# Two Trainium2 routing hand-overs: first-layer expert weights released in halves, and a GpSimd bias add moved behind them

## The chip, the cores and the metric

The kernel runs on one core of one Trainium2 chip. The metric is device time in microseconds (us) of one execution; lower is better. The five engines run their own instruction streams and meet only through semaphores: TensorE (PE in the profile; its weight loads are PEld), VectorE (DVE), ScalarE (ACT), GpSimd (POOL) and SyncE (SP), which issues the transfers.

## The reference, cut to what matters

The input x is 4 rows (sequences) of 512 tokens with 512 features. The model is a block of two feed-forward layers around an attention-like layer:

```
x = x + 0.5 * ffn(layernorm(x))
x = x + attn(layernorm(x))
x = x + 0.5 * ffn(layernorm(x))

ffn(x):
    logits = x.reshape(4, 512*512) @ switch_w.T + switch_b     # one routing decision per row
    gate, top_idx = top_k(softmax(logits), 2)                  # 2 of 8 experts per row
    for each of 16 heads of 32 features and both chosen experts k:
        h = gelu(x_head @ w1[k].T + b1[k])                     # 32 -> 32
        o += gate[k] * (h @ w2[k].T + b2[k])                   # 32 -> 32
    return (x + o) @ w3.T + b3
```

So each feed-forward layer begins with a routing decision that needs the whole normalised input, and no expert matmul can start before the decision for its row is known.

## The kernel before, in words

**Precision.** Matmuls are made of three products: an operand is split in a rounded high part (type `F32R`) and the remainder, its low part, and hi*hi, hi*lo and lo*hi are summed in PSUM.

**The two routings.** All four rows are routed together. In the first phase `route(0)` multiplies the normalised x with `switch_w` (512 matmuls); VectorE's `choose` then reads the result from PSUM, sums it (`part`, L1254), spreads it by row (`lmix`, L1255), TensorE sums over the partitions (L571), and `choose` goes on to `place`, the rank of each expert in each row. ScalarE takes the exponential meanwhile. `select(row, f, 0)` then picks the first-layer weights of the row's two experts from a table and writes them as a block diagonal for two heads at a time; `select(row, f, 1)` does the same for the second layer, and its column 32 is the bias b1 (semaphore `s_b1`). `gate`, called in the middle of it, makes the gates. The third phase, with the second feed-forward layer, repeats all this after the attention of the last row as `route(1)`, `logits(1)`, `choose(1)`.

**Feed-forward work.** f counts the feed-forward layers of rows: 0 to 3 the first, 4 to 7 (B = 4 and more, "late") the second. The features lie in KC = 4 chunks c of 128. TensorE's `hidden(f, c)` makes the hidden values of both experts in two PSUM banks: two matmuls for each of its three products. ScalarE's `gelu` reads them (it needs `s_b1`), `second_hi` or `hidden_hi` rounds; VectorE's `split_hidden` (f below 4) casts `h_hi` of k = 0 (L1357) and subtracts for `h_lo` (L1358, twice), `hidden_lo` does the subtractions alone (L1364). TensorE's `experts_out(f, c)` (O0 to O3; L436 to L438, six matmuls each) waits for `s_hl`, one count for each `h_lo`. `z_out` on ScalarE and `z_split` on VectorE (L1376) bring its result out of PSUM, and `w3_tile` (W0 to W3) multiplies by w3. VectorE's `w3_add` (L1383) adds what GpSimd has left in `xa`.

**What GpSimd does here.** `residual_bias(f, t)` (L1148) adds half of b3 to a 128x512 tile of the normalised layer's input, in place, and signals `s_xb`, which `w3_add` waits for. In the first routing its four adds for f = 0 start as soon as the last tile is normalised; for f = B they start when the four `xt_lo` tiles of that layer are written.

**Order of the work.** Each engine's order is written out by hand. Around the first routing VectorE does: `route_norm`, four `xt_split`, `choose(0)`, `select(0, 0, 0)`, `select(0, 0, 1)` with `gate(0)`, `split_hidden(0, 0)`, `split_hidden(0, 1)`, the low part of w3 (`w3_lo`, L1513, 128x2048), then `split_hidden(0, 2)`, `z_split(0, 0)`, `split_hidden(0, 3)` and the other `z_split`. TensorE does: `hidden(0, 0)`, `hidden(0, 1)`, O0, `hidden(0, 2)`, O1, `hidden(0, 3)`, O2, six matmuls of `w3_ahead`, O3, `w3_behind`. Around the second routing VectorE does: `choose(1)`, `select(0, B, 0)`, `select(0, B, 1)`, `hidden_lo(B, 0)`, `normalise(B + 1, 1)` (L1337), `hidden_lo(B, 1)`, `z_split(B, 0)`, `select(1, B + 1, 0)`, `hidden_lo(B, 2)`, `z_split(B, 1)`, `xt_split`, `select(1, B + 1, 1)`, `hidden_lo(B, 3)`.

**Steps.** `own.do(ins)` issues a VectorE instruction and waits for it on VectorE's own semaphore; `own.mark` only counts it. `VE_ROW_STEPS` is the count of such steps in the loop over the middle rows.

Of the kernel before, what the change touches and what calls it, by code (L numbers as in the profile page):

```python
# [31 lines left out]
P = 128  # L32
ALU = mybir.AluOpType
# [6 lines left out]
B, S, D = 4, 512, 512  # L40
NT = S // P
KC = D // P
E, TOPK = 8, 2
HD = 32
# [12 lines left out]
PAIR = 2  # L57
# [33 lines left out]
def macaron_kernel(nc, x, w_in, w_out, switch_w, tables_in, w3, out):  # L91
    x2_dram = nc.dram_tensor("x2_dram", (B, S, D), F32).ap()

    with ExitStack() as ctx:
        def sb(name, shape, dt=F32, into=ctx):
            return into.enter_context(nc.sbuf_tensor(name, shape, dt))

        def sem(name):
            return ctx.enter_context(nc.semaphore(name))
# [43 lines left out]
        with ExitStack() as region:  # L143
# [4 lines left out]
            w_diag = sb("w_diag", [P, TOPK, PAIR, HD], into=region)  # L148
# [12 lines left out]
        xt_hi = sb("xt_hi", [P, KC, S], F32R)  # L161
        xt_lo = sb("xt_lo", [P, KC, S], F32R)
# [43 lines left out]
        pair_of = sb("pair_of", [P, PAIR])  # L206
# [31 lines left out]
        def weights(of):  # L238
# [3 lines left out]
                    xt_lo=xt_lo, prod=prod, w_diag=w_diag)  # L242
        late0 = dict(ffn0, prod=prod_late, w_diag=w_diag_late)
        late1 = dict(weights(set1), z_hi=z_hi1, z_lo=z_lo1, xt_hi=xt_hi1,
                     xt_lo=xt_lo1, prod=prod_late, w_diag=w_diag_late)
# [6 lines left out]
        def is_late(f):  # L252

            return isinstance(f, int) and f >= B

        def ffn_set(f):
            return (late1 if f % 2 else late0) if is_late(f) else ffn0
# [69 lines left out]
        s_sh = sem("s_sh")  # L327
        s_exp = sem("s_exp")
        s_sel = [sem("s_sel1"), sem("s_sel2")]
        s_b1 = sem("s_b1")  # L330

        s_xn = sem("s_xn")
# [7 lines left out]
        s_hl = sem("s_hl")  # L340
# [81 lines left out]
        def normed(n):  # L422

            _, t, lo, hi = EVENTS[n]
            if n < FEW + 2:
                return n + 1
            assert n >= LAST
            return n - 1
# [111 lines left out]
        def _(pe):  # L540
# [56 lines left out]
            def hidden(f, c, after_row):  # L597
                use = ffn_set(f)
                if c == 0:
                    pe.wait_ge(s_sel[0], f + 1)  # L600
                pe.wait_ge(s_t1e, KC * f + c + 1)
                pe.wait_ge(s_xtl, KC * f + c + 1)
                for k in range(PAIR):
                    if after_row is not None and c == 0:
                        pe.wait_ge(s_ina, OUT_JOBS * after_row + 15 + k)
                    elif not (isinstance(f, int) and f == 0 and c == 0):
                        pe.wait_ge(s_gelu, H_JOBS * f + PAIR * (c - 1) + k + 1)
                half = [slice(k * HALF, (k + 1) * HALF) for k in range(PAIR)]
                dst = [h_bank[k][:] for k in range(PAIR)]
                for k in range(PAIR):  # L610
                    pe.matmul(dst[k], use["w1_hi"][half[k], :], use["xt_hi"][half[k], c, :], start=True, stop=False)  # L611
                for k in range(PAIR):
                    pe.matmul(dst[k], use["w1_lo"][half[k], :], use["xt_hi"][half[k], c, :], start=False, stop=False)
                for k in range(PAIR):
                    pe.matmul(dst[k], use["w1_hi"][half[k], :], use["xt_lo"][half[k], c, :], start=False,  # L615
                              stop=True).then_inc(s_h, 1)

            def experts_out(f, c):
# [129 lines left out]
            def row_end(b):  # L748
# [24 lines left out]
                t1(f, 2, b, False)  # L773
                t1(f, 3, b, False)
                hidden(f, 0, b)
                for name in ("A0", "A1"):
                    do(name, range(KC - 1, KC))
                hidden(f, 1, b)
                do("A2", range(1))
                do("O0")  # L780
                hidden(f, 2, b)
                do("O1")
                hidden(f, 3, b)
# [313 lines left out]
        def _(pool):  # L1097
            own = Steps(pool, s_po)
# [45 lines left out]
            def residual_bias(f, t):  # L1144

                ap = ffn_input(f)[0][:, t, :]
                pool.wait_ge(s_xn, NT * f + t + 1)
                pool.tensor_tensor(ap, ap, b3_half, ALU.add).then_inc(s_xb, 1)  # L1148
# [16 lines left out]
            pool.wait_ge(s_b3, 1)  # L1165
            pool.wait_ge(s_x0, NT - 1)
            pool.wait_ge(s_rn, normed(NT - 1))
            for t in range(NT):
                residual_bias(0, t)
            ln_rstd(0)  # L1170
# [11 lines left out]
            pool.memset(set1[4][:].bitcast(F32), 0.0).then_inc(s_pad, 1)  # L1182
            pool.memset(set1[5][:].bitcast(F32), 0.0).then_inc(s_pad, 1)
            pool.wait_ge(s_xtl, KC * (B + 1))
            for c in range(KC):
                residual_bias(B, c)
            for f in range(B + 1, 2 * B):
# [9 lines left out]
        def _(ve):  # L1197
            own = Steps(ve, s_ve)
# [6 lines left out]
            def route_stats(n):  # L1205

                phase, t, lo, hi = EVENTS[n]
                src = route_src(n)
                if lo == 0:
                    if phase == 0:  # L1210
                        ve.wait_ge(s_xc[t], 16)
                    else:
                        ve.wait_ge(s_xr[t % 2], 16 * (t // 2 + 1))
                for b in range(lo, hi):
                    m = own.mark(ve.bn_stats(stats[:, b, :], src(b)))
                return m
# [72 lines left out]
            def select(row, f, n, gates=lambda: None):  # L1289

                use = ffn_set(f)
                w_diag = use["w_diag"]
                if n == 0:
                    prod, out = use["prod"][:, :, 0:HD, :], use["sel"][0]
                    for k in range(TOPK):
                        m = own.mark(ve.scalar_tensor_tensor(
                            out=prod[:, k], in0=place[:, bass.ds(row, 1), :].to_broadcast([P, HD, E]),
                            scalar=float(k), in1=tab[0][:, 0:HD, :], op0=ALU.is_equal, op1=ALU.mult))
                    own.wait(m)
                    for k in range(TOPK):  # L1300
                        m = own.mark(ve.tensor_reduce(out[:, k, :], prod[:, k], AX.X, ALU.add))
                    own.wait(m)
                    for k in range(TOPK):
                        m = own.mark(ve.tensor_tensor(
                            w_diag[:, k], out[:, k, :].unsqueeze(1).to_broadcast([P, PAIR, HD]),
                            pair_of[:].unsqueeze(2).to_broadcast([P, PAIR, HD]), ALU.mult))
                    own.wait(m)
                    full = w_diag[:].rearrange("p k j c -> p (k j c)")
                    hi, lo = use["w1_hi"][:], use["w1_lo"][:]
                else:  # L1310
                    prod, out = use["prod"][:, 0], use["sel"][1]
                    own.do(ve.scalar_tensor_tensor(
                        out=prod, in0=place[:, bass.ds(row, 1), :].to_broadcast([P, FB, E]), scalar=half_of[:],
                        in1=tab[1], op0=ALU.is_equal, op1=ALU.mult))
                    ve.tensor_reduce(out[:], prod, AX.X, ALU.add).then_inc(s_b1, 1)
                    gates()
                    ve.wait_ge(s_b1, f + 1)
                    own.do(ve.scalar_tensor_tensor(
                        out=w_diag[:, 0], in0=out[:, 0:HD].unsqueeze(1).to_broadcast([P, PAIR, HD]),
                        scalar=gate_p[:, bass.ds(row, 1)], in1=pair_of[:].unsqueeze(2).to_broadcast([P, PAIR, HD]),  # L1320
                        op0=ALU.mult, op1=ALU.mult))
                    if is_late(f):
                        ve.wait_ge(s_pad, 2)
                    full = w_diag[:, 0].rearrange("p j c -> p (j c)")
                    hi, lo = use["w2_hi"][:, 1, :], use["w2_lo"][:, 1, :]
                    if not isinstance(f, int):
                        own.mark(ve.tensor_copy(b2_row[:], b2_col[:, bass.ds(row, 1)]))
                own.do(ve.tensor_copy(hi, full))
                ve.tensor_tensor(lo, full, hi, ALU.subtract).then_inc(s_sel[n], 1)  # L1329
                ve.wait_ge(s_sel[n], f + 1)  # L1330

# [174 lines left out]
            ve.wait_ge(s_pc, 1)  # L1506
            choose(0)
            select(0, 0, 0)
            select(0, 0, 1, lambda: gate(0))
            split_hidden(0, 0, None)  # L1510
            split_hidden(0, 1, None)
# [63 lines left out]
            with ve.Fori(1, B - 1) as b:  # L1575
                own.base, own.n = base + (b - 1) * VE_ROW_STEPS, 0
                row(b)
                assert own.n == VE_ROW_STEPS, own.n

            own.base, own.n = base + (B - 2) * VE_ROW_STEPS, 0  # L1580

# [11 lines left out]
            for t in range(NT):  # L1593
                out_add(t, job_last(f"A{t}"), last_bank[t], x1, x1)
                ve.wait_ge(s_obf, job_last(f"A{t}") + 1)
                m = route_stats(LAST + t)
# [41 lines left out]
                w3_add(2 * B - 1, t, job_late(2 * B - 1, f"W{t}"), out_bank(f"W{t}"))  # L1638


VE_ROW_STEPS = 56


# [34 lines left out]
```

## Time and profile before

| | us |
|---|---|
| median of 3 runs (lowest, highest) | 535.35 (534.96, 535.4) |
| the profiled execution's own time | 535.08 |
| its span in the trace | 533.3 |
| TensorE matmul busy | 487.2 (91% of the span) |
| VectorE busy | 415.1 (78%) |
| ScalarE busy | 220.0 (41%) |
| GpSimd busy | 104.1 (20%) |

The span is that of the instructions in the trace; 1.8 us of the execution's time lie around it. A row of the timeline gives the start in us from the span's start, the duration in us, the engine, line, operation, tiles and forms, and how many instructions were merged in the row; in brackets stands the idle time of the engine before it and what ended it. The granted clock of TensorE is given as a share of full speed: 1.00 is 2.4 GHz, 0.50 is 1.2 GHz.

### The profile page before, as it was taken

The numbers are of one execution on the slowest core, as the hardware profiler recorded it, in microseconds if no ns is written. First come the engines' busy times: TensorE is split into PE (matmuls) and PEld (weight loads), VectorE is DVE, ScalarE is ACT, GpSimd is POOL, SyncE is SP. The second block draws the span as 40 slices with busy tenths as digits, with TensorE's granted clock in tenths as the row PEclk, the third lists the DMA queues.
The fourth block names the chain that finished last, engine by engine and source line by source line (L and its number), as shares of the span: only waits on it lengthen the run. The fifth ranks groups of instructions, "written<-read, shape, count | busy, mean of one in ns | idle before, by whom it ended". The sixth has DMA issues, their size and how long they took to land.

```text
span 533.3 us, 8582 instructions
## 1 busy us (share of the span) xinstructions
PE 487.2 (91%) x3184; PEld 353.9 (66%) x3204; DVE 415.1 (78%) x801; ACT 220.0 (41%) x352; POOL 104.1 (20%) x116
## 2 busy tenths in 40 slices
PE   0566999999999999999999999999999748999997
PEld 0553676667687666768666677866667635777775
DVE  3878888999875599887569979758997679878642
ACT  0226753444714222572422257141344238665630
POOL 5150036000013500001440000154121320021220
PEclk9786999999999999999999999999999978999999
DMA  8999020000102000010200001034665060131112
GB/s 335 409 371 417 10 79 2 1 1 0 41 20 100 0 1 0 2 40 21 98 0 0 0 0 39 20 138 166 235 226 202 4 206 33 41 111 47 60 59 80
DMA packets 16370, 48.19 MB, mean 90 GB/s; under 512 B 1232, under 2 KB 1232, under 8 KB 14544
## 3 DMA queue, kind: packets, MB, share of 16 engines
q1 hardware_dynamic: 16336, 47.73, 24.2%
q8 instruction: 22, 0.36, 0.3%
q14 instruction: 12, 0.10, 0.1%
HBM read 39.34 MB, written 8.39 MB: 89 GB/s over the span
## 4 chain that ended last, share of the span: by engine, by line
PE 73%; DVE 12%; issue 5%; SPq 3%; DMA 3%; POOL 2%; ACT 1%; POOLq 0%; DVEq 0%; ACTq 0%
PE bank L436 11%; PE bank L438 10%; PE bank L437 10%; PE bank L739 8%; PE bank L740 8%; PE bank L742 8%; DMA route_w<-in_switch_w 3%; SPq L462 2%; PE bank L611 2%; PE bank L593 2%; PE bank L703 2%; PE bank L706 2%; PE bank L711 2%; PE bank L562 2%; POOL rs L1159 2%
## 5 line engine op out<-in xcount | busy, mean ns | idle before, releaser
L739 PE MATMUL bank<-xh,win_hi 128*128 128x512 f32 x256 | 112.6, 440 | 0.0
L740 PE MATMUL bank<-xl,win_hi 128*128 128x512 f32 x256 | 100.6, 393 | 0.0
L742 PE MATMUL bank<-xbf,win_lo 128*128 128x512 bf16 x240 | 65.9, 381 | 1.0
L739 PEld LDWEIGHTS bank<-xh,win_hi 128*128 128x128 f32 x256 | 48.2, 188 | 15.9 <-DVE qn L1447 0.2
L1153 POOL TENSOR_TENSOR rstd<-mv,neg_half 128x1 f32<-128x1 f32 x16 | 9.6, 597 | 246.1 <-DVE mv L1408 246.1
L740 PEld LDWEIGHTS bank<-xl,win_hi 128*128 128x128 f32 x256 | 48.2, 188 | 10.1
L1159 POOL TENSOR_TENSOR rs<-ms,neg_half 128x16 f32<-128x16 f32 x16 | 46.6, 2933 | 23.9 <-DVE ms L1442 23.9
L436 PE MATMUL bank<-w_hi,z_hi 128*128 128x512 f32 x124 | 50.1, 404 | 0.0
L438 PE MATMUL bank<-w_hi,z_lo 128*128 128x512 f32 x124 | 48.5, 391 | 0.0
L437 PE MATMUL bank<-w_lo,z_hi 128*128 128x512 f32 x124 | 48.5, 391 | 0.0
L742 PEld LDWEIGHTS bank<-xbf,win_lo 128*128 128x128 bf16 x256 | 21.1, 98 | 30.7 <-issue 17.4
L877 ACT ACTIVATE hf<-bank,w_sel 128x512 f32<-128x512 f32 x52 | 33.0, 687 | 13.3 <-PE bank L615 9.6
L1148 POOL TENSOR_TENSOR xa<-xa,tables 128x512 f32<-128x512 f32 x16 | 20.2, 1278 | 63.4 <-DVE x L1383 46.2
L1383 DVE TENSOR_TENSOR x<-bank,xa 128x512 f32<-128x512 f32 x28 | 19.3, 690 | 16.2 <-PE bank L438 16.2
L902 ACT ACTIVATE z_hi<-bank,b_col 128x512 fp32r<-128x512 f32 x24 | 16.5, 686 | 31.2 <-PE bank L438 31.2
L436 PEld LDWEIGHTS bank<-w_hi,z_hi 128*128 128x128 f32 x124 | 23.3, 188 | 8.5 <-issue 4.0
L928 ACT ACTIVATE xh<-bank 128x512 fp32r<-128x512 f32 x16 | 9.6, 600 | 46.2 <-PE bank L692 46.2
L1376 DVE SCALAR_TENSOR_TENSOR z_lo<-bank,b_col,z_hi 128x512 fp32r<-128x512 f32 x24 | 17.9, 749 | 13.3 <-ACT z_hi L902 13.1
L611 PE MATMUL bank<-xt_hi,w_hi 64*128 64x512 f32 x64 | 17.5, 542 | 11.7 <-DVE w_lo L1329 8.6
L436 PE MATMUL bank<-wo_hi,y_hi 128*128 128x512 f32 x64 | 27.0, 421 | 0.0
L942 ACT ACTIVATE y_hi<-yt 128x512 fp32r<-128x512 f32 x16 | 10.1, 631 | 40.8 <-DVE yt L1478 40.8
L438 PEld LDWEIGHTS bank<-w_hi,z_lo 128*128 128x128 f32 x124 | 23.3, 188 | 5.2
(217 smaller groups left out, 1060.2 us busy)
## 6 DMA issues: line engine op xcount, KB each, us to landing
route_w<-in_switch_w SPq DMA_DIRECT2D x14, 512.0 KB, 14.0
route_w<-in_switch_w SPq DMA_DIRECT2D x5, 1024.0 KB, 4.7
xa<-in_x SPq DMA_DIRECT2D x4, 1024.0 KB, 5.2
route_w<-in_switch_w SPq DMA_DIRECT2D x2, 2048.0 KB, 15.6
out<-x SPq DMA_DIRECT2D x16, 256.0 KB, 2.0
x_dram<-x1p SPq DMA_DIRECT2D x12, 256.0 KB, 2.0
xa<-x_dram SPq DMA_DIRECT2D x3, 1024.0 KB, 5.7
x_chunk<-in_x SPq DMA_DIRECT2D x2, 1024.0 KB, 17.7
```

The lines of the kernel that those rows point to most:

```text
L436: pe.matmul(res, a_hi, b_hi, start=start, stop=False, skip_group_check=onto)
L437: pe.matmul(res, a_hi, b_lo, start=False, stop=False, skip_group_check=onto)
L438: return pe.matmul(res, a_lo, b_hi, start=False, stop=stop, skip_group_check=onto)
L611: pe.matmul(dst[k], use["w1_hi"][half[k], :], use["xt_hi"][half[k], c, :], start=True, stop=False)
L739: pe.matmul(bank[:], win_hi[:, c, r, k, :], xh[:, k, :], start=(k == 0), stop=False)
L740: pe.matmul(bank[:], win_hi[:, c, r, k, :], xl[:, k, :], start=False, stop=False)
L742: mm = pe.matmul(bank[:], win_lo[:, c, r, k, :], xbf[:, k, :], start=False, stop=(k == KC - 1))
L877: act.activation(hid_set(f, c)[0][:, k, :], h_bank[k][:], ACT.Gelu, bias=ffn_set(f)["sel"][1][:, HD:FB]).then_inc(s_gelu, 1)
L1148: pool.tensor_tensor(ap, ap, b3_half, ALU.add).then_inc(s_xb, 1)
L1159: pool.tensor_tensor(rs[:, t, :], ms[:, t, :], neg_half[:], ALU.pow).then_inc(s_rs, 1)
L1376: ve.scalar_tensor_tensor(out=use["z_lo"][:, c, :], in0=bank[:], scalar=b2_of(f), in1=use["z_hi"][:, c, :], op0=ALU.add, op1=ALU.subtract) ...
L1383: ve.tensor_tensor(x1[:, t, :], bank[:], ffn_input(f)[0][:, t, :], ALU.add).then_inc(s_obf, 1)
```

## The change

Three things are changed.

1. `select(..., 0)` wrote the masked selection to `w_diag` with two instructions of 128x64 (one for each expert), cast it into `w1_hi`, subtracted for `w1_lo`, and signalled once. Now one instruction over 128x128 writes the masked product directly to `w1_hi` (rounded on the way out) and signals a new semaphore `s_sel1h`; a second one writes the same product unrounded to `w_diag`, and the subtraction follows.
2. `hidden` waits for `s_sel1h` before its first matmuls, does hi*hi and hi*lo(x) first and waits for `s_sel[0]` before the two matmuls with `w1_lo`, which come last.
3. GpSimd's four adds of b3 for f = 0 wait in addition until four `h_lo` tiles are written, and those for f = B until `normalise(B + 1, 1)` is done.

```diff
             def hidden(f, c, after_row):
                 use = ffn_set(f)
                 if c == 0:
-                    pe.wait_ge(s_sel[0], f + 1)
+                    pe.wait_ge(s_sel1h, f + 1)
...
                 for k in range(PAIR):
                     pe.matmul(dst[k], use["w1_hi"][half[k], :], use["xt_hi"][half[k], c, :], start=True, stop=False)
                 for k in range(PAIR):
-                    pe.matmul(dst[k], use["w1_lo"][half[k], :], use["xt_hi"][half[k], c, :], start=False, stop=False)
+                    pe.matmul(dst[k], use["w1_hi"][half[k], :], use["xt_lo"][half[k], c, :], start=False, stop=False)
+                if c == 0:
+                    pe.wait_ge(s_sel[0], f + 1)
                 for k in range(PAIR):
-                    pe.matmul(dst[k], use["w1_hi"][half[k], :], use["xt_lo"][half[k], c, :], start=False,
+                    pe.matmul(dst[k], use["w1_lo"][half[k], :], use["xt_hi"][half[k], c, :], start=False,
                               stop=True).then_inc(s_h, 1)
...
             pool.wait_ge(s_b3, 1)
             pool.wait_ge(s_x0, NT - 1)
             pool.wait_ge(s_rn, normed(NT - 1))
+            pool.wait_ge(s_hl, 2 * TOPK)
             for t in range(NT):
                 residual_bias(0, t)
...
             pool.wait_ge(s_xtl, KC * (B + 1))
+            pool.wait_ge(s_xn, NT * (B + 2))
             for c in range(KC):
                 residual_bias(B, c)
...
                         m = own.mark(ve.tensor_reduce(out[:, k, :], prod[:, k], AX.X, ALU.add))
                     own.wait(m)
-                    for k in range(TOPK):
-                        m = own.mark(ve.tensor_tensor(
-                            w_diag[:, k], out[:, k, :].unsqueeze(1).to_broadcast([P, PAIR, HD]),
-                            pair_of[:].unsqueeze(2).to_broadcast([P, PAIR, HD]), ALU.mult))
-                    own.wait(m)
+                    wide = [P, TOPK, PAIR, HD]
+                    columns = out[:].unsqueeze(2).to_broadcast(wide)
+                    own_half = pair_of[:].unsqueeze(1).unsqueeze(3).to_broadcast(wide)
+                    hi, lo = use["w1_hi"][:], use["w1_lo"][:]
+                    ve.tensor_tensor(hi.rearrange("p (k j c) -> p k j c", k=TOPK, j=PAIR), columns, own_half,
+                                     ALU.mult).then_inc(s_sel1h, 1)
+                    own.do(ve.tensor_tensor(w_diag[:], columns, own_half, ALU.mult))
                     full = w_diag[:].rearrange("p k j c -> p (k j c)")
-                    hi, lo = use["w1_hi"][:], use["w1_lo"][:]
+                    ve.wait_ge(s_sel1h, f + 1)
...
-                own.do(ve.tensor_copy(hi, full))
+                if n == 1:
+                    own.do(ve.tensor_copy(hi, full))
                 ve.tensor_tensor(lo, full, hi, ALU.subtract).then_inc(s_sel[n], 1)
...
-VE_ROW_STEPS = 56
+VE_ROW_STEPS = 54
```

## Rows read from the trace of the kernel before

**Rows 1.** The page: busy time, and engines in the chain that ended last.
```profile
PE 487.2 (91%) x3184; PEld 353.9 (66%) x3204; DVE 415.1 (78%) x801; ACT 220.0 (41%) x352; POOL 104.1 (20%) x116
...
PE 73%; DVE 12%; issue 5%; SPq 3%; DMA 3%; POOL 2%; ACT 1%; POOLq 0%; DVEq 0%; ACTq 0%
```

**Rows 2.** Windows: stretch, length, PE, PEld, DVE, ACT, POOL busy (count), PEclk, DMA, GB/s.
```profile
43.30:50.90 7.60, 6.06 (x18) 3.54 (x18) 6.42 (x20) 3.79 (x6) 0.00 (x0) 0.50 1.02 430
...
444.00:455.00 11.00, 9.51 (x52) 6.62 (x51) 10.65 (x24) 10.62 (x20) 0.00 (x0) 1.00 0.01 2
```

**Rows 3.** Timeline of POOL and DVE around both routings' b3 adds.
```profile
33.55 4.95 POOL L1148 TENSOR_TENSOR xa<-xa,tables 128x512 f32<-128x512 f32 x4 [1.88 <-DVE xnr L1241]
...
37.25 1.26 POOL L1148 TENSOR_TENSOR xa<-xa,tables 128x512 f32<-128x512 f32 x1
...
33.24 2.47 DVE L1369 TENSOR_TENSOR xt_lo<-bank,xt_hi 128x512 fp32r<-128x512 f32 x4
...
38.01 0.55 DVE L1255 TENSOR_TENSOR lmix<-part,row_of 128x32 f32<-128x32 f32 x1
...
424.62 4.94 POOL L1148 TENSOR_TENSOR xa<-xa,tables 128x512 f32<-128x512 f32 x4 [4.28 <-DVE xt_lo L1369]
...
428.94 0.67 DVE L1255 TENSOR_TENSOR lmix<-part,row_of 128x32 f32<-128x32 f32 x1
```

**Rows 4.** Timeline of DVE, first routing.
```profile
40.18 0.19 DVE L1268 TENSOR_TENSOR lg<-lg,red 128x32 f32<-128x32 f32 x1
...
42.33 0.36 DVE L1304 TENSOR_TENSOR w_diag<-w_sel,pair_of 128x64 f32<-128x64 f32 x2
42.72 0.23 DVE L1328 CAST w_hi<-w_diag 128x128 fp32r<-128x128 f32 x1
42.98 0.29 DVE L1329 TENSOR_TENSOR w_lo<-w_diag,w_hi 128x128 fp32r<-128x128 f32 x1
...
43.84 0.43 DVE L1315 TENSOR_REDUCE w_sel<-prod 128x33 f32<-128x264 f32 x1
...
48.86 0.43 DVE L1357 CAST h_hi<-hf 128x512 fp32r<-128x512 f32 x1 [0.63 <-ACT hf L877]
...
50.78 2.28 DVE L1513 SCALAR_TENSOR_TENSOR w_lo<-w_raw,w_hi 128x2048 fp32r<-128x2048 f32 x1
52.98 0.42 DVE L1357 CAST h_hi<-hf 128x512 fp32r<-128x512 f32 x1
53.43 1.31 DVE L1358 TENSOR_TENSOR h_lo<-hf,h_hi 128x512 fp32r<-128x512 f32 x2
```

**Rows 5.** Timeline of PE, first routing.
```profile
43.33 0.79 PE L611 MATMUL bank<-xt_hi,w_hi 64*128 64x512 f32 x2 [4.31 <-DVE w_lo L1329]
...
48.06 0.79 PE L436 MATMUL bank<-h_hi,w_hi 128*128 128x512 f32 x1
...
54.35 0.50 PE L436 MATMUL bank<-h_hi,w_hi 128*128 128x512 f32 x1
...
57.65 0.39 PE L436 MATMUL bank<-h_hi,w_hi 128*128 128x512 f32 x1
```

**Rows 6.** Timeline of POOL and DVE in the first row's attention.
```profile
83.22 3.39 POOL L1159 TENSOR_TENSOR rs<-ms,neg_half 128x16 f32<-128x16 f32 x1
...
80.34 2.90 POOL L1159 TENSOR_TENSOR rs<-ms,neg_half 128x16 f32<-128x16 f32 x1 [0.36 <-DVE ms L1442]
...
81.57 2.29 DVE L1486 TENSOR_TENSOR win_lo<-raw_y,win_hi 128x2048 bf16<-128x2048 f32 x1
```

**Rows 7.** Timeline of DVE and PE, second routing.
```profile
439.27 1.91 DVE L1337 TENSOR_SCALAR xnw<-xa,mv,rstd 128x512 f32<-128x512 f32 x4
...
442.85 0.75 DVE L1376 SCALAR_TENSOR_TENSOR z_lo<-bank,b_col,z_hi 128x512 fp32r<-128x512 f32 x1 [0.46 <-ACT z_hi L902]
...
446.06 1.29 DVE L1364 TENSOR_TENSOR h_lo<-hf,h_hi 128x512 fp32r<-128x512 f32 x2
...
451.07 0.50 PE L436 MATMUL bank<-h_hi,w_hi 128*128 128x512 f32 x1 [1.28 <-DVE h_lo L1364]
```

More of the change, by code:

```diff
@@ L329, in macaron_kernel @@
         s_sel = [sem("s_sel1"), sem("s_sel2")]
+        s_sel1h = sem("s_sel1h")
         s_b1 = sem("s_b1")
```

## The prediction

> **What bounds the kernel now.** I read the page first: TensorE is busy 91% of the span and is 73% of the chain that ended last, VectorE 12% [rows 1]. Time is won or lost only where TensorE waits or runs at its low clock, and both routings are such places. In the first, TensorE stands idle 4.31 us until VectorE's `w_lo` [rows 5]; from there to 50.9 us its granted clock is 0.50, the 1.2 GHz level [rows 2]. After the second, in 444 to 455 us, VectorE is busy 10.65 of 11.00 us, and the experts' last output waits 1.28 us for a VectorE subtraction [rows 2, 7]. From there TensorE has work without a gap, so what is gained or lost at these two places stays to the end. At six other `select` calls the weights are ready long before TensorE asks.
>
> **The port that the adds hold.** The timeline of VectorE and GpSimd together shows why the adds matter. L1255, 128x32 with two inputs in SBUF, takes 0.55 and 0.67 us; L1268 of the same form takes 0.19 [rows 3, 4]. Both times GpSimd's fourth b3 add is running, and L1255 ends just behind it: 38.56 against 38.51, and 429.61 against 424.62 + 4.94 = 429.56 [rows 3]. The reverse is there too: the reciprocal root on GpSimd at 83.22 takes 3.39 us where its neighbour takes 2.90, and L1486 (two SBUF inputs, 2.29 us) ran until 83.86 [rows 6]. The four L1369, with one input in PSUM, keep a pace of 0.62 us beside the adds [rows 3]. So I read that a VectorE instruction with two SBUF inputs and a GpSimd add exclude each other, and whoever comes second waits for the other to finish.
>
> **Part 1, the adds taken away from `choose`.** L1255 falls to 0.19: -0.36 us in the first routing, -0.48 in the second, on the path both times.
>
> **Part 2, the early high part.** Before, from the start of the two L1304 (42.33) to TensorE's start (43.33) is 1.00 us [rows 4, 5]. Now TensorE waits for one 128x128 product, priced as L1329 of the same size, 0.29, plus the 0.06 that TensorE's start lay behind L1329's end: 0.35, a gain of 0.65. The trace has no such product with broadcast inputs; it can't be below half of the L1304 pair's 0.36 nor much above all of it, and 0.29 lies between. The low part: two products at a step of about 0.21, a gap of 0.04 and L1329 make 0.83, against 0.94 before; VectorE is 0.11 ahead. TensorE asks for it after four matmuls, about 1.02 us at the low clock, 1.37 us after L1304's old start; it is there after 0.89, so the new wait costs nothing (TensorE's queue behind it holds the last two matmuls and O0, which gain nothing by passing it). The gelu needs b1 from L1315, then at 44.27 - 0.47 = 43.80, also earlier. So the hidden values come 0.65 + 0.36 = 1.0 us earlier in the first routing and 1.13 in the second.
>
> **What of it arrives.** First routing: VectorE is only 0.47 ahead when it starts on `h_lo`, so O0 starts 0.84 us early instead of 1.0 (47.2 against 48.06 [rows 5]). That work is done at the low clock; taking the clock's rise to stay at 50.9, 0.84 us more at half rate leave about 0.45. Second routing: VectorE bounds, not TensorE. `hidden_lo(B, 0)` moves by 1.06, one more `select` gives another 0.11: -1.17. Without any new contention the sum is -0.45 - 1.17 = -1.6 us. The six other `select` calls give 0.1 us of VectorE each, hidden behind TensorE's matmuls; if that cover were missing they would give 0.6 in all.
>
> **Part 3, where the adds go.** Four adds hold 4.95 us of GpSimd [rows 3]. By the rows one add holds VectorE off for about 1.1 us: it starts at 37.25, and L1255 with 0.19 of its own must have started at 38.37. In the first routing `s_hl` reaches four at 49.85 (the splits of c = 1 waited for the gelu [rows 4], so they move by the full 1.0), just as VectorE starts `w3_lo`, 2.28 us with two SBUF inputs, 49.77 to 52.05. GpSimd waits that out. VectorE's next, the cast of c = 2 (0.42 us for 512 elements where the subtraction needs 0.69, so it too moves more than one element at a time) must wait for the gelu until about 52.2, so add 1 is in first and holds until 53.1. I let them alternate, since each leaves a gap: VectorE waits for its own semaphore between cast and subtraction, and GpSimd's next add starts reading only after the last has ended. Then cast 53.1 to 53.5, add 2 to 54.6, the two subtractions to 55.3 and 55.9 (before: 54.12 and 54.74). O2 starts at 55.35 instead of 54.35 [rows 5]. Add 3 runs beside `z_split` and holds the next cast until 56.95; cast to 57.4; add 4 to 58.5; the first `h_lo` of c = 3 at 59.2. O3 starts at 59.25 instead of 57.65: **+1.6 us**, the gains included. The sums themselves are wanted only by `w3_add` after O3, and are not late.
>
> Second routing: `normalise` ends at 441.18 - 1.06 = 440.1 [rows 7]. The two subtractions of c = 1 are already issued and run 1.2 us more, to 441.25; add 1 lies beside idle time and `z_split` (0.75, one input in PSUM), free. Add 2 lies beside the two reductions of `select(1, B + 1, 0)` and holds the first product 0.3 us; add 3 holds the low-part subtraction 1.07; add 4 holds `hidden_lo(B, 2)`, at 446.06 before, 1.07. If add 2 wins against the first instruction of `select` the same sum comes out in another order. That is +2.44 - 1.17, or **+1.25 us** at the subtraction that O3 waits for [rows 7].
>
> Sum: 1.6 + 1.25 = 2.85. Against the profiled execution that is 535.08 + 2.85 = 537.9; the median is 0.27 higher, so 538.2. The bounds of the cost per add: nothing, and its full step of 1.24.
>
> The Trainium skill has a rule on this (page "SBUF — State Buffer", section "Who interferes with whom"): the shared pair of ports is an exclusive lock, whoever issues first has it for the whole instruction, and a VectorE instruction with two SBUF inputs, or a cast in a two-port mode, is blocked fully. L1255 agrees to 0.05 us. By that page with 1.24 for each hold the sum would be about 0.6 us larger; the rows say 1.1, and I keep that.
>
> **Rivals.**
> (a) The adds don't hold long VectorE instructions. For it: at 81.57 L1486 runs its 2.29 us beside GpSimd's 2.90 us root with no loss [rows 6], so GpSimd doesn't bar VectorE through all of an instruction. Against it: the root reads 16 elements and then computes, the add reads 512 all through, and L1255 stood still twice to the end of one. It decides if casts and subtractions beside the moved adds keep 0.42 and 0.69. Then only the gain is left: 535.35 - 1.6 = 533.7, or 533.3 where the clock rises earlier with the work. Faster.
> (b) GpSimd doesn't get into the 0.03 us gaps between dependent VectorE instructions, only beside PSUM ones and idle time. Then in the first routing add 1 holds the cast, the subtraction ends at 54.25 and O2 starts as before; the others lie beside `z_split`: 0. Second routing: 0.3 + 0.6 - 1.17 = -0.3. Together 535.05: no change.
> (c) GpSimd keeps the port for four adds in a row. The cast of c = 2 starts 4.9 us after 52.05: O2 at 58.1, +3.7; in the second routing `select` stands until 446.1, 3.65 - 1.17 = +2.5. 541.5.
> Nothing in the change can fail to happen: the waits are new and the high part is signalled apart.
>
> **How the numbers follow.** Alternating 0.56, with its own range 536.6 to 540.3 (per-add hold 0.8 to 1.24, one place more or less where two take turns); (c) 0.08; (a) 0.20; (b) 0.16. The predicted time is 538.2. The range is 533.6 to 540.5: it takes in (a) and (b) and leaves out (c) and the edges. About 0.2% (1.1 us) is what this kernel's measurement can tell from no change. Faster 0.20; same 0.16; slower 0.64.
>
> **What would show it.** Right: L1255 at 0.19 twice; TensorE's L611 behind the masked product and not `w_lo`, with no idle before the last pair; the first b3 add stretched to over 3 us while L1513 runs; at least two of L1357 and L1358 behind it at 1.4 to 1.8 us instead of 0.42 and 0.69; TensorE idle about 1 us before O2 and before O3; the same on the subtractions after 443 us. Wrong: all adds at 1.26 and VectorE rows unchanged beside them (a); or stretched VectorE instructions that TensorE doesn't wait for, because it was still further behind at the low clock than I take it.

## The result, and the profile after

The changed kernel takes 538.56 us (median of 6 runs, 537.14 to 540.13), the kernel before 535.2 (6 runs, 534.34 to 535.4): ratio 1.0071, 95% interval 1.0061 to 1.0081, or 3.8 us slower. 538.2 was predicted. The profiled execution took 538.79 us, with a span of 537.1. The runs lie up to 3.0 us apart, those of before 1.1. Below, a hold is the time by which a VectorE instruction lasts longer beside a GpSimd add than without one.

Both gains that the change can bring are in the trace. Timeline of VectorE, first routing, changed kernel:

```profile
37.94 0.19 DVE L1260 TENSOR_TENSOR lmix<-part,row_of 128x32 f32<-128x32 f32 x1
...
41.89 0.29 DVE L1312 TENSOR_TENSOR w_hi<-w_sel,pair_of 128x128 fp32r<-128x128 f32 x1
42.10 0.28 DVE L1314 TENSOR_TENSOR w_diag<-w_sel,pair_of 128x128 f32<-128x128 f32 x1
42.42 0.29 DVE L1337 TENSOR_TENSOR w_lo<-w_diag,w_hi 128x128 fp32r<-128x128 f32 x1
...
49.69 2.28 DVE L1521 SCALAR_TENSOR_TENSOR w_lo<-w_raw,w_hi 128x2048 fp32r<-128x2048 f32 x1
51.89 1.52 DVE L1365 CAST h_hi<-hf 128x512 fp32r<-128x512 f32 x1
53.44 1.63 DVE L1366 TENSOR_TENSOR h_lo<-hf,h_hi 128x512 fp32r<-128x512 f32 x1
...
54.99 1.77 DVE L1366 TENSOR_TENSOR h_lo<-hf,h_hi 128x512 fp32r<-128x512 f32 x1
...
57.35 0.83 DVE L1365 CAST h_hi<-hf 128x512 fp32r<-128x512 f32 x1
```

`lmix` takes 0.19 us instead of 0.55, and TensorE starts right behind the first product (below), 0.35 us after it begins, where it was 1.00 before. Then come the adds. The cast of c = 2 takes 1.52 instead of 0.42, the two subtractions 1.63 and 1.77 instead of 0.69, the cast of c = 3 0.83 instead of 0.42 [rows 4]. The adds themselves, timeline of GpSimd:

```profile
50.03 3.09 POOL L1151 TENSOR_TENSOR xa<-xa,tables 128x512 f32<-128x512 f32 x1 [18.35 <-DVE h_lo L1366]
...
53.08 1.44 POOL L1151 TENSOR_TENSOR xa<-xa,tables 128x512 f32<-128x512 f32 x1
...
54.49 1.73 POOL L1151 TENSOR_TENSOR xa<-xa,tables 128x512 f32<-128x512 f32 x1
...
56.17 1.73 POOL L1151 TENSOR_TENSOR xa<-xa,tables 128x512 f32<-128x512 f32 x1
```

One alone takes 1.26 [rows 3]. The first starts while L1521 runs to 51.97, waits it out, and ends at 53.12; the cast can only end behind it, at 53.41. Then they take turns: the second add ends at 54.52, the first subtraction at 55.07, the third add at 56.22, the second subtraction at 56.76. What TensorE sees of it:

```profile
42.24 0.80 PE L612 MATMUL bank<-xt_hi,w_hi 64*128 64x512 f32 x2 [3.65 <-DVE w_hi L1312]
42.83 0.63 PE L614 MATMUL bank<-xt_lo,w_hi 64*128 64x512 f32 x2
43.26 0.63 PE L618 MATMUL bank<-xt_hi,w_lo 64*128 64x512 f32 x2
...
55.12 0.50 PE L437 MATMUL bank<-h_hi,w_hi 128*128 128x512 f32 x1 [1.90 <-DVE h_lo L1366]
...
56.82 0.80 PE L437 MATMUL bank<-h_hi,w_hi 128*128 128x512 f32 x1 [0.72 <-DVE h_lo L1366]
57.41 0.63 PE L438 MATMUL bank<-h_lo,w_hi 128*128 128x512 f32 x1
...
60.29 0.39 PE L437 MATMUL bank<-h_hi,w_hi 128*128 128x512 f32 x1
```

The last pair of `hidden` follows with no idle time: the low part is not late. O2 starts at 55.12 (54.35 before) and its second half at 56.82, behind 1.90 and 0.72 us of idle time. From 56.82 a matmul takes 0.63 us instead of 0.39: the granted clock has fallen to 0.50, the 1.2 GHz level, a second time (0.50 over 57 to 59 us). The same stretch in windows:

```profile
53.00:56.00 3.00, 1.10 (x5) 0.49 (x3) 2.97 (x3) 2.15 (x4) 3.00 (x3) 1.00 0.05 19
56.00:57.00 1.00, 0.28 (x2) 0.18 (x2) 1.00 (x2) 0.00 (x0) 1.00 (x2) 0.61 0.00 0
57.00:60.00 3.00, 3.00 (x8) 2.38 (x9) 2.96 (x5) 1.49 (x2) 0.90 (x1) 0.56 0.00 0
```

TensorE (first column after the length) was busy 1.10 of 3.00 us before the fall; the eighth column, counted with the stretch as the first, is the clock. O3 starts at 60.29, 2.64 us later than before [rows 5]. It doesn't wait for VectorE there: the first `h_lo` of c = 3 is done at 58.91 (58.22 + 0.69), and TensorE's own matmuls run up to O3 without idle time, most of them at the low clock.

Second routing, timeline of VectorE, GpSimd and TensorE:

```profile
431.50 0.19 DVE L1260 TENSOR_TENSOR lmix<-part,row_of 128x32 f32<-128x32 f32 x1
...
444.94 1.85 DVE L1301 SCALAR_TENSOR_TENSOR prod_late<-place,tables 128x256 f32<-128x256 f32 x2
446.82 0.74 DVE L1306 TENSOR_REDUCE w_sel<-prod_late 128x32 f32<-128x256 f32 x2
447.60 0.49 DVE L1312 TENSOR_TENSOR w_hi<-w_sel,pair_of 128x128 fp32r<-128x128 f32 x1
448.01 1.35 DVE L1314 TENSOR_TENSOR w_diag_late<-w_sel,pair_of 128x128 f32<-128x128 f32 x1
...
442.80 6.42 POOL L1151 TENSOR_TENSOR xa<-xa,tables 128x512 f32<-128x512 f32 x4 [19.96 <-issue]
...
450.47 0.50 PE L437 MATMUL bank<-h_hi,w_hi 128*128 128x512 f32 x1 [2.31 <-DVE h_lo L1372]
...
454.73 0.50 PE L437 MATMUL bank<-h_hi,w_hi 128*128 128x512 f32 x1 [1.27 <-DVE h_lo L1372]
```

VectorE's products in `select` (L1301, L1312, L1314) are held, by 1.10, 0.20 and 1.07 us; the reductions (0.74) are not. O2 waits 2.31 us for the low part behind them, O3 1.27. `choose(1)` began 2.56 us later than before and the O3 of [rows 7] starts 3.66 later, so the second routing costs 1.10 us net. From there to the end is 82.4 us, as before (82.2).

### The profile page after: what moved, and what is told of

Read it like the earlier page. It is cut to its first block, busy times and chain, and to the rows that moved or that the text cites. A ratio compares the mean times of both kernels' runs of the same rounds, so it can differ in the third digit from the quotient of the medians.

```text
span 537.1 us, 8598 instructions
## 1 busy us (share of the span) xinstructions
PE 489.8 (91%) x3204; PEld 354.9 (66%) x3204; DVE 419.1 (78%) x793; ACT 220.3 (41%) x352; POOL 108.5 (20%) x116
## 4 chain that ended last, share of the span: by engine, by line
PE 73%; DVE 16%; issue 5%; POOL 4%; ACT 1%; POOLq 0%; DVEq 0%; ACTq 0%
PE bank L437 11%; PE bank L439 10%; PE bank L438 10%; PE bank L742 8%; PE bank L743 8%; PE bank L745 8%; PE bank L594 3%; PE bank L612 2%; PE bank L706 2%; PE bank L709 2%; PE bank L714 2%; PE bank L563 2%; POOL rs L1162 2%; DVE stats L1220 1%; PE bank L618 1%
## 5 line engine op out<-in xcount | busy, mean ns | idle before, releaser
L745 PE MATMUL bank<-xbf,win_lo 128*128 128x512 bf16 x256 | 69.0, 382 | 0.0
L1151 POOL TENSOR_TENSOR xa<-xa,tables 128x512 f32<-128x512 f32 x16 | 24.6, 1554 | 79.5 <-DVE x L1391 30.3
L437 PE MATMUL bank<-h_hi,w_hi 128*128 128x512 f32 x52 | 23.2, 445 | 6.4 <-DVE h_lo L1372 3.6
```

What stands on the lines that cost most here:

```text
L437: pe.matmul(res, a_hi, b_hi, start=start, stop=False, skip_group_check=onto)
L745: mm = pe.matmul(bank[:], win_lo[:, c, r, k, :], xbf[:, k, :], start=False, stop=(k == KC - 1))
```

## The experiments

The table has one row for each kernel. "First" is from the start of `choose(0)` to the start of the last `z_split` of f = 0; "second" is from the start of `choose(1)` to 82.3 us before the end of the span. Both are of one profiled execution each, so they carry the spread of single executions; the medians and ratios do not come from them. Kernels are best compared by the ratio, since the median of before differs by up to 0.3 us between batches.

| kernel | median us (runs) | ratio to before, 95% | first | second |
|---|---|---|---|---|
| before | 534.9 to 535.0 in the batches below | | 22.48 | 22.6 |
| changed | 538.56 (6) | 1.0071 (1.0061 to 1.0081) | 25.19 | 23.8 |
| halves only | 533.99 (7) | 0.9975 (0.9964 to 0.9986) | 22.95 | 21.5 |
| late adds only | 540.19 (6) | 1.0108 (1.0083 to 1.0132) | 26.14 | 24.6 |
| first adds late | 537.12 (5) | 1.0048 (1.0035 to 1.0061) | 24.31 | 22.1 |
| second adds late | 536.9 (5) | 1.0037 (1.0024 to 1.005) | 21.69 | 25.0 |
| thin adds | 532.73 (5) | 0.996 (0.9947 to 0.9973) | 21.81 | 21.4 |
| half adds | 533.81 (11) | 0.9981 (0.9972 to 0.999) | 22.39 | 21.9 |
| fourth add moved, halves | 532.23 (6) | 0.9955 (0.9942 to 0.9967) | 21.63 | 21.2 |
| fourth add moved only | 533.92 (11) | 0.9982 (0.9973 to 0.9991) | 22.82 | 22.0 |
| changed, filled wait | 539.84 (6) | 1.0101 (1.0084 to 1.0118) | 24.09 | 24.0 |
| changed, second profile | 539.86 (1) | | 25.29 | 24.8 |
| changed, third profile | 539.0 (1) | | 24.90 | 24.8 |

**The halves only.** The changed kernel, with GpSimd as before:

```diff
-            pool.wait_ge(s_hl, 2 * TOPK)
...
-            pool.wait_ge(s_xn, NT * (B + 2))
```

> The changed kernel without the two added GpSimd waits: the b3 adds run where they ran before, only the early high part is left. If the loss comes from the adds holding VectorE off: L1255's successor (L1260) is back at about 0.55 and 0.67 us, all casts and h_lo subtractions at 0.42 and 0.69, and the kernel is about 1.0 us faster than before (0.3 in the first routing, where VectorE and the low clock keep most of the 0.65; 0.65 to 0.7 in the second): about 534.2. If the early high part or the new order of hidden's matmuls were the cause of the loss: slower than before, towards 538.

1.3 us faster by the ratio. The early high part and the new order of the matmuls are not what costs. With the adds back in their place `lmix` is stretched again, to 0.60 and 0.40 us (timeline of VectorE, both routings):

```profile
38.00 0.60 DVE L1258 TENSOR_TENSOR lmix<-part,row_of 128x32 f32<-128x32 f32 x1
...
429.29 0.40 DVE L1258 TENSOR_TENSOR lmix<-part,row_of 128x32 f32<-128x32 f32 x1
```

**The late adds only.** The kernel before with the two waits added:

```diff
             pool.wait_ge(s_rn, normed(NT - 1))
+            pool.wait_ge(s_hl, 2 * TOPK)
...
             pool.wait_ge(s_xtl, KC * (B + 1))
+            pool.wait_ge(s_xn, NT * (B + 2))
```

> The kernel before with only the two GpSimd waits added. If the adds are the cause: L1255 at 0.19 twice, the same stretched casts and subtractions as in the changed kernel, and the loss of the changed kernel plus what the early high part gave: 539.3 (4 us slower than before). If the loss needs the early high part too (the adds falling on other work because everything moved): less than 2 us slower.

1.08% slower, 5.8 us by the ratio, where 4 were expected; the interval is wide, 4.4 to 7.1 us. The holds are the same without the other half of the change (the cast 1.52 us, the pair of subtractions 3.33), so they don't hang on what the early high part moved. The profile shows the second fall of the clock too, behind 1.69 and 0.74 us of idle time, and "first" is 26.14.

**Each routing alone.** One of the two added waits taken out of the changed kernel.

> The changed kernel with only the first routing's adds moved. The two traces give 2.6 us lost in the first routing and 1.1 in the second. If the two places are independent: 535.2 + 2.6 - 0.7 = 537.1. If what is lost in the first is given back later, or the second is the larger: below 536.

> The changed kernel with only the second routing's adds moved. Independent places: 535.2 - 0.4 + 1.1 = 535.9. TensorE never waits in the first routing behind a stretched VectorE instruction, and its clock is not lowered again near 57 us. If the second place were the main cause: over 537.

The first came out as expected (537.12 against 537.1), but its profiled execution took 535.77, the lowest of the five: that profile, in which the clock doesn't fall a second time, is not one of a median run. The second was a miss: 536.9 against 535.9. In its profile (536.18 us) the first routing gives 0.8 us instead of 0.4, and the second costs 2.4 instead of 1.1. Timeline of TensorE:

```profile
446.60 0.79 PE L437 MATMUL bank<-h_hi,w_hi 128*128 128x512 f32 x1 [3.41 <-DVE h_lo L1371]
447.19 0.63 PE L438 MATMUL bank<-h_lo,w_hi 128*128 128x512 f32 x1
```

The idle time before O2 is 3.41 us instead of 2.31, because TensorE got there earlier, and behind it the clock is at the low level for the six matmuls of O2 and what follows. O2 starts 19.41 us after `choose(1)`, as in the first profile of the changed kernel (19.48), O3 24.69 instead of 23.74. "Second" is 25.0 us there, against 23.8 in that profile, where the clock did not fall.

**Thin adds.** The changed kernel with the same waits and the same eight instructions, over one column, so that b3 is left out of the other 511:

```diff
-                pool.tensor_tensor(ap, ap, b3_half, ALU.add).then_inc(s_xb, 1)
+                if isinstance(f, int) and f in (0, B):
+                    pool.tensor_tensor(ap[:, 0:1], ap[:, 0:1], b3_half[:, 0:1], ALU.add).then_inc(s_xb, 1)
+                else:
+                    pool.tensor_tensor(ap, ap, b3_half, ALU.add).then_inc(s_xb, 1)
```

> The changed kernel with the eight moved adds cut to one column of 512 (b3 is left out of the other 511 columns for f = 0 and f = B). The same waits, the same count of GpSimd instructions, hardly any reading. If VectorE is held off by the adds' reading: casts and subtractions at 0.42 and 0.69, no idle time of TensorE before O2, and all of the forecast gain, about 1.6 us: 533.6. If the waits or their signals cost the time: as slow as the changed kernel, 538 to 539.

532.73: faster than before by 0.4%, and by 5.8 us than the changed kernel. Casts and subtractions are back at their own times (timeline of VectorE):

```profile
51.93 0.43 DVE L1368 CAST h_hi<-hf 128x512 fp32r<-128x512 f32 x1
52.39 0.69 DVE L1369 TENSOR_TENSOR h_lo<-hf,h_hi 128x512 fp32r<-128x512 f32 x1
```

Neither the waits nor the signals cost anything; what the adds do over their columns does.

**Half adds.** The same with `0:D // 2`, 256 of the 512 columns.

> The changed kernel with the eight moved adds over 256 of 512 columns (b3 is left out of the other half for f = 0 and f = B). Thin adds measured 2.2 us faster than before, full ones 3.7 slower. If the cost goes with how long each add holds VectorE off: holds of about 0.5 us, and about half of the 5.9 us between them, 535.7. If it is a cost for each of the eight adds whatever its length: near 538.5. If half an add fits into the idle and PSUM time in between: near 533.

A miss, and a useful one: 533.81, not 535.7. The holds did go with the length (the cast 0.95, so 0.53 held; the pair 2.25, so 0.94 for two), but their price did not: half the length costs 1.1 us more than none, the full length 5.8. TensorE waits 0.82 and 0.17 us before the two halves of O2 instead of 1.90 and 0.72, no cast of c = 3 is held, and there is no second fall of the clock in this profile. Holds are paid for only beyond the slack of what waits behind them, and here without the low clock.

**Only the fourth add moved.** In both routings `lmix` met the fourth add alone. It is moved to where VectorE has idle time or inputs in PSUM; the other three stay where they were before (the edit against the kernel before):

```diff
             for t in range(NT):
+                if t == NT - 1:
+                    pool.wait_ge(s_obf, NT - 1)
                 residual_bias(0, t)
...
             for c in range(KC):
+                if c == KC - 1:
+                    pool.wait_ge(s_hl, H_JOBS * (B + 1) + TOPK)
                 residual_bias(B, c)
```

With the early high part and its new order of matmuls, and without the two waits of the change:

> The early high part, three of four adds of each routing where they were before, and only the fourth (the one L1255 met) moved: in the first routing behind the third z_split, where VectorE is idle 1.41 us, in the second behind hidden_lo(B + 1, 0), in front of two instructions with an input in PSUM and 0.56 us of idle. If the hold is all there is to it: L1255's successor at 0.19 twice, no VectorE instruction stretched, 533.6 (1.6 us faster than before). If GpSimd's adds cost whatever they lie beside: not faster than the halves alone.

532.23, the fastest kernel here: 0.45% faster than before, 6.3 us faster than the changed one. Timeline of VectorE and GpSimd in it:

```profile
57.74 1.29 POOL L1151 TENSOR_TENSOR xa<-xa,tables 128x512 f32<-128x512 f32 x1 [20.45 <-DVE z_lo L1386]
...
59.06 0.75 DVE L1386 SCALAR_TENSOR_TENSOR z_lo<-bank,b_col,z_hi 128x512 fp32r<-128x512 f32 x1 [1.40 <-ACT z_hi L905]
...
427.64 0.19 DVE L1262 TENSOR_TENSOR lmix<-part,row_of 128x32 f32<-128x32 f32 x1
```

The add fits into the 1.40 us before the last `z_split`, and `lmix` is free.

The same move in the kernel before, without the early high part:

> The kernel before with only its fourth b3 add of each routing moved to the places of the kernel that has both; no early high part. The halves alone measured 0.9 us, both together 2.7. If the two gains add, this one is worth 1.8 us, 533.1, which is more than the 0.84 us that L1255 loses by its own duration; if the two need each other, it gives 0.84 or less, 534.1.

1.0 us faster (ratio 0.9982; 0.5 to 1.4 us by the interval), so near the 0.84 that `lmix` loses, and not 1.8. By the ratios the two gains add within the noise: 0.25% and 0.18% apart, 0.45% together. The 1.8 had been taken from a difference of medians (0.9 us for the halves), which the ratio puts at 1.3.

**The clock.** Eight matmuls in TensorE's queue, with no reader, to fill its wait before O2:

```diff
                 if c == KC - 1:
                     w3_ahead()
+                if c == 2:
+                    for i in range(8):
+                        pe.matmul(o_bank[1][:], xt_hi[:, 0, 0:P], xt_hi[:, i % 4, :], start=True, stop=True)
                 experts_out(0, c)
```

> The changed kernel with eight matmuls of 128x512 put into TensorE's queue in front of O2, into a PSUM bank that nobody reads then; they fill the 1.9 us in which it waits there. If about 1 us of the first routing's loss is the clock falling to 1.2 GHz at 56.8 us behind these idle times: the granted clock stays up to 60 us, O3 starts up to 1 us earlier than in the changed kernel, 537.6 or less, and the runs lie closer together. If the clock is not what costs: same as the changed kernel, or later by what the matmuls take beyond the wait.

In its profile the clock stays up through the first routing and "first" is 24.09 us instead of 25.19. The whole kernel is not faster, though: 539.84, slower than the changed kernel by the ratios (1.0101 against 1.0071, with intervals that don't meet), and the runs lie no closer together (538.91 to 541.62). So the expectation failed for the total, while the part that it was about behaved in one profile. Where the rest goes is open. The same profile takes 369.3 us between the two stretches instead of 368.4. In its second routing the clock falls too, at about 451.6 us, behind 2.53 us of idle time before O2; it costs little there (O3 starts 23.82 us after `choose(1)`, against 23.74), since it runs into idle time before O3. This run does not settle what the fall costs. Two more profiles of the changed kernel itself:

> The changed kernel, unchanged, for a second look at its clock. Its first profile shows the granted clock fall to 0.50 again for 3 us behind the idle time before O2, and the first routing took 25.19 us from choose to the last z_split; the kernel with only the first adds moved has the same stretched instructions, no such fall, and took 24.31. If the fall is worth about 0.9 us: a look without it shows 24.1 to 24.5, one with it 25 or more.

> The changed kernel once more, a third look at the same thing: 24.1 to 24.5 from choose to the last z_split where the clock doesn't fall a second time, 25 or more where it does; the stretched VectorE instructions are the same in every look, to 0.1 us, if they are holds and not chance.

Neither was without the fall: "first" is 25.29 and 24.90, so all three profiles of the changed kernel have it and the comparison within one kernel is missing for the first routing. Across kernels: first adds late, with the same pair of subtractions (3.35 us), has no fall and 24.31. Timeline of TensorE there:

```profile
57.17 0.50 PE L437 MATMUL bank<-h_hi,w_hi 128*128 128x512 f32 x1 [0.73 <-DVE h_lo L1365]
...
59.48 0.40 PE L437 MATMUL bank<-h_hi,w_hi 128*128 128x512 f32 x1
```

These are the starts of O2's second half and of O3. The nine matmuls from one to the other take 2.31 us there; in the three profiles of the changed kernel they take 3.47, 3.58 and 3.18, and 3.74 with the late adds only. The stretched instructions repeat (cast 1.51 and 1.52, pair 3.33 and 3.32): they are not chance.

The second routing is new: in both profiles the clock falls there too, and "second" is 24.8 instead of 23.8. Timeline of TensorE, second profile:

```profile
450.36 0.80 PE L437 MATMUL bank<-h_hi,w_hi 128*128 128x512 f32 x1 [3.55 <-DVE h_lo L1372]
450.95 0.63 PE L438 MATMUL bank<-h_lo,w_hi 128*128 128x512 f32 x1
```

The first low stretch had ended earlier there (the clock is 0.66 over 435 to 445 us, against 0.51 in the first profile), so TensorE came to its wait earlier and stood 3.55 us in it instead of 2.31. VectorE has the low part ready at the same time: O2 starts 19.48, 19.39 and 19.39 us after `choose(1)` in the three profiles. O3 starts 23.74 us after it in the first, 24.68 and 24.67 in the other two. So the same kernel costs about 0.9 us more in executions in which the clock falls right behind that wait. These two executions took 539.86 and 539.0 us, above the median.

## Why the prediction was right, point by point

**What each add holds.** Predicted about 1.1 us, from `lmix` alone. Measured: the first cast 1.10, the two subtractions 0.94 and 1.08, `select` 1.10 and 1.07. Right; where an add was already well on its way the hold is shorter (the cast of c = 3 0.41, L1312 0.20). The rival that long VectorE instructions aren't held (0.20) fell with the first profile, and thin adds confirm it: with one column left of each add, nothing is held and the kernel is fast.

**Taking turns.** Right, and more strictly than assumed: the third add came between the two subtractions of c = 2, which are issued back to back, while I had let VectorE keep the port for the pair. That delayed O2's second half (56.82, against 56.15 by the prediction's 55.35 and the 0.80 between the halves before); the fourth add held the cast of c = 3, and its subtraction was spared. Four in a row (0.08) and only in long gaps (0.16) are out.

**The first routing, predicted +1.6, measured +2.64.** O2 was placed at 55.35 and came at 55.12. The step from there to O3 is wrong in two ways. The wait: O3 was to stand behind VectorE's first `h_lo` of c = 3, at 59.2, with TensorE idle before it. That `h_lo` came at 58.91, and O3 had no idle time before it; it stood behind TensorE's own matmuls, which began with O2's late second half. The term that is missing is the clock: idle times of 1.90 and 0.72 us were followed by the low level from 56.8 to about 59.5. Without it those nine matmuls would take 2.31 us (first adds late) instead of 3.47, and O3 would start at about 59.1, an estimate, near the predicted 59.25 but for another reason. Compared from `choose(0)` on, the two kernels differ by about 0.9 us (25.19 against 24.31), as far as two single executions show it.

**The second routing, predicted +1.25, measured +1.10** in the profile, with holds of 2.37 us against 2.44. They fell on the first products of `select` and not on `hidden_lo(B, 2)`, an order that the prediction had left open with the same sum. In two other profiles it was about 1 us more, with the clock's fall. The gain in it, predicted as 1.17 us with the 0.48 of `lmix` in it, comes out at 1.2 (thin adds) to 1.4 us (fourth add moved): "second" falls from 22.6 to 21.4 and 21.2 us when nothing is held.

**The gain without holds, predicted 1.6 us, measured 2.1 (thin adds) to 2.4 (fourth add moved).** The term that was too small is the 0.45 us of the first routing. It rested on the clock's rise staying at 50.9 us. It does not stay: over 50 to 60 us the granted clock is 0.95 before, 0.99 in the kernel with the fourth add moved and the halves, 1.00 with the second adds late, 0.87 with the halves only and 0.89 with the fourth add moved only, and "first" follows it: 22.48, 21.63, 21.69, 22.95, 22.82. Windows of the halves only:

```profile
50.00:60.00 10.00, 9.87 (x41) 6.35 (x39) 8.05 (x11) 7.73 (x11) 0.00 (x0) 0.87 0.26 111
```

In that execution the gain of 0.65 us was more than eaten. The medians are taken over executions of either sort.

**The total, 538.2 against 538.56** (2.85 us of loss forecast, 3.8 by the ratio), is therefore right in the mechanism of the holds and in most of its terms, with one term missing and one too small, of opposite effect: about +0.9 to +2 for the clock's falls and -0.5 to -0.8 for the gain. That the number came within 0.4 us is in part luck, since these two offset each other.

**The adds being wanted late.** Right: GpSimd is done at 57.9 and 449.2, well before `w3_add`, and the thin adds show that the waits themselves are free.

## What to carry to other kernels

Before an add is moved off one stalled VectorE instruction, list every VectorE instruction that will then run beside it and ask of each whether it has two SBUF inputs or is an SBUF cast; a hold lasts to the end of GpSimd's add, however short the VectorE instruction is (`lmix`, 0.19 us, took 0.55 and 0.67). Move only the one that is in the way, and put it beside instructions that read PSUM, reductions, or idle time. And price idle time of TensorE above its length: where the wait was followed by the low clock, 0.9 us or so was added to it, and 0.1 in the one case where the low clock ran into more idle time (second routing with the filled wait). The kernels with such waits also had the wider spread of runs (3.0 us for the changed one against 1.1); that the clock makes this spread is not shown.

## What the runs showed of the hardware

- Two VectorE instructions issued back to back do not keep a GpSimd add out: 1.63 and 1.77 us for two subtractions of 0.69.
- A cast of 128x512 from SBUF to SBUF (0.42 us) is held like an instruction with two SBUF inputs (1.52 us). That is the rule of the Trainium skill (page "SBUF — State Buffer", section "Who interferes with whom") for its two-port modes, and the trace agrees; it also names reductions as free, and L1306 keeps its 0.74 us beside the adds.
- The hold is nearer to 1.1 than to the add's recorded 1.26 us, and 0.5 for half the columns.
- TensorE's clock fell from 1.00 to 0.50 in all three profiles of the changed kernel's first routing, behind idle times of 1.90 and 0.72, 1.79 and 0.72, and 2.20 us (there it fell inside O2's first half, before the next 0.41), and behind 1.69 and 0.74 us with the late adds only. Behind 0.97 and 0.73 us (first adds late) and 0.82 and 0.17 us (half adds) it stayed.
- In the second routing it fell behind 3.41, 3.55 and 3.58 us (second adds late, and two profiles of the changed kernel) and behind 2.53 us in the kernel with the filled wait; behind 2.31 us (first profile of the changed kernel) and 2.45 us (late adds only) it stayed.
